# Dividing the softmax's exponentials by their sum on GpSimd instead of VectorE, in a cross-attention block of float32 products

## The chip, the core and the metric

The kernel is one program on one core of one Trainium2 chip. The metric is the device time of one execution in microseconds (us); before the change its median over 3 runs is 2565.36 us (2563.90 to 2565.37).

## The reference: what is computed

The input is x of 8 x 256 x 512 and a context of the same size, both float32. A first block (phi, theta, g and w are 1x1 convolutions, then a fixed batch normalisation) gives a new x without a softmax. Then come two cross-attention layers with 16 heads of size 128 and an MLP of width 2048, each behind a layer norm and each added to x. The part that the change touches is the softmax of the attention:

```
qh = (q_in @ wq + bq).reshape(b, q_len, H, K)
kh = concatenate([(kv_in @ wk + bk)..., bias_k]);  vh = concatenate([(kv_in @ wv + bv)..., bias_v])
logits  = einsum('bqhk,bthk->bhqt', qh, kh) / sqrt(K)
weights = softmax(logits, axis=-1)
ctx     = einsum('bhqt,bthk->bqhk', weights, vh)
return ctx.reshape(b, q_len, H * K) @ wo + bo
```

There are 256 queries and 256 keys (and one bias key) for each pair of a batch element and a head.

## The kernel before

**Products in two parts.** Each float32 operand is held as two tensors, `_hi` (rounded to the fast matmul's format) and `_lo` (what is left), and each product is three matmuls: hi*hi, lo*hi, hi*lo (`product`, L488 to L492). So whoever makes an operand makes it twice: ScalarE writes the `_hi` part out of PSUM, and VectorE then writes the `_lo` part as a difference.

**Loops.** The batch is worked on in 2 halves of 4 elements (8 tiles of 128 tokens). A half runs the first block, then 2 layers of 8 bodies, then 8 MLP bodies. An attention body handles two heads; it is one of FIRST, MIDDLE (6 of the 8), LAST and FINAL, so that the kernel has 24 MIDDLE bodies and 8 others. FIRST and LAST or FINAL also hold half of a layer norm each.

**Items.** A body has 8 items, one for each head and batch element, numbered j = 0 to 7. An item goes through these steps:

- L_j on TensorE: the logits into `S` (L639)
- the row maximum `mx` (L1015) and its negative multiple `nm` (L1017) on VectorE
- two exponentials on ScalarE into `probs`, with the row sums (L805)
- `divide` on VectorE: one reciprocal of the sums into `rs` (L1023), then for each of two tiles of 128 queries a multiplication of `probs` by `rs` (L1026), 128x256 each
- T_j on TensorE: four transposes of `probs` into `T` (L647), which wait for the semaphore a_prob
- `PT_hi` on ScalarE (L813) and `PT_lo` on VectorE (L1031)
- P_j on TensorE: the product with the values into `O`, which waits for `PT_lo` (L655)
- `oT_hi` on ScalarE (L818) and `oT_lo` on VectorE (L1037)

**Filler.** Between these steps TensorE computes units, the projections of the next operands: q, k, v for this body, K and V for the next, and w, the output product that is added to x (L1004). For a v unit VectorE adds a bias into `tmp` (L948), ScalarE makes `v_hi` and VectorE `v_lo` (L952). The order is written out by hand in a string for each kind of body, and every engine follows it in its own queue, without exceptions. A piece of it for MIDDLE, where each u is half a unit:

```
MIDDLE: "uuuu L0 uuu L1 T0 uu P0 u L2 T1 uu P1 u L3 T2 uu P2 u L4 T3 uu P3 u L5 T4 ..."
```

VectorE takes an item's steps so: at T_j it makes PT_lo of item j and then divides item j+1, and at L_j it takes the maximum of item j.

**GpSimd** (POOL) splits the weights: for each of wos, wks, wvs and wqs a cast of 128x1024 (L399) and a subtraction of 128x1024 (L401), when the last unit that reads the old weights is done and the load has landed. For wvs a third operation makes the value bias `vb` (L406). SyncE loads the next weights into `raw_ok` and `raw_vq` when a split is done. In the bodies with a layer norm GpSimd also computes the reciprocal standard deviation (`rsqrt`, L417) and adds the output bias to four tiles of x (`add_bias`, L424); VectorE makes the normalised `z` (L908) and `hT_lo` (L969) there.

Of the kernel before, what the change touches and what calls it, by code (L numbers as in the profile page):

```python
# [30 lines left out]
ALU = mybir.AluOpType  # L31
# [21 lines left out]
ITEMS = 8  # L53
# [4 lines left out]
FIRST, MIDDLE, LAST, FINAL = range(4)  # L58
# [9 lines left out]
def units_of(kind):  # L68

    return [u for u in UNITS_A if kind != FINAL or u[0] not in "KV"]  # L70


def per_body(what, kind=MIDDLE):

    return sum(u[0] in what for u in units_of(kind))


def before(half, e, what):

    return half * ((HBODIES - 1) * per_body(what) + per_body(what, FINAL)) + e * per_body(what)  # L80
# [97 lines left out]
def bass_xattn(nc, x_in, ctx_in, thw, thb, pgw, pgb, www, bncol, wa, wk, wv, wb, hcol, vrow,  # L178
               lncol, f1col, orow, out):
    ctx = ExitStack()  # L180
    with ctx:
        def sb(name, shape, dt=F32):
            return ctx.enter_context(nc.sbuf_tensor(name, [P, *shape], dt))
# [5 lines left out]
        def sem(name):  # L189
            return ctx.enter_context(nc.semaphore(name))  # L190

        def f(ap):

            return ap.bitcast(F32)
# [28 lines left out]
        probs = sb("probs", [2, 2, 258])  # L223
# [19 lines left out]
        rs = sb("rs", [2, 2])  # L243
# [41 lines left out]
        a_rawmax, a_max, a_exp, a_rcp, a_prob = (sem("a_" + s) for s in ("rawmax", "max", "exp", "rcp", "prob"))  # L285
# [25 lines left out]
        def wait_apart(eng, sem, value):  # L311


            eng.wait_ge(sem, value)
            eng.sem_inc(apart, 1)
# [65 lines left out]
        def _(pool):  # L381
# [11 lines left out]
            def as_out(raw):  # L393
                return raw[:].rearrange("p (c a) n -> p c (a n)", c=2)

            def halve(hi_lo, raw, m, count, hi_count):

                wait_apart(pool, raw_in[m], count)
                pool.tensor_copy(hi_lo[0][:], raw).then_inc(hi_part, 1)  # L399
                pool.wait_ge(hi_part, hi_count)  # L400
                return pool.tensor_tensor(hi_lo[1][:], raw, f(hi_lo[0][:]), ALU.subtract)  # L401

            def halve_v(done, hi_count):

                halve(wvs, raw_vq[:], "v", done * 32, hi_count)
                return pool.tensor_tensor(vb[:], raw_vb[:, 0, :], raw_vb[:, 1, :], ALU.subtract)  # L406
# [7 lines left out]
            def rsqrt(l, p):  # L414

                pool.wait_ge(ln_eps, l * 2 + p + 1)
                pool.tensor_tensor(rstd[:], vpe[:], minus_half[:], ALU.pow).then_inc(ln_rstd, 1)  # L417

            def add_bias(l, p):

                pool.wait_ge(brow_in, l * 16 + 16)
                for t in range(4 * p, 4 * p + 4):
                    pool.wait_ge(ln_z, l * TILES + t + 1)
                    pool.tensor_tensor(x[:, t, :], x[:, t, :], brow[:], ALU.add).then_inc(ln_bias, 1)  # L424

            def attention(half, layer, g, kind):
                e = layer * BODIES + g
                n = pool.snap(half * HBODIES + e)
                E = pool.snap(half * STREAM + e)
                hi0 = pool.snap(half * HI_HALF + e * 4 + HI0)  # L430
                l = half * NORMS + layer
                units = units_of(kind)
                ub = pool.snap(before(half, e, ALL))
                if kind == FIRST:
                    rsqrt(l, 1)

                pool.wait_ge(a_unit, ub + CR1)
                pool.wait_ge(m_unit, half * (MUNITS * MBODIES) + CR1)
                halve(wos, as_out(raw_ok), "o", E * 16 + 16, hi0 + 1).then_inc(split["o"], 1)
                if kind == FIRST:  # L440
                    add_bias(l, 1)

                pool.wait_ge(a_unit, ub + units.index(("k", 1, 1)) + 1 + CR1)
                halve(wks, raw_ok[:], "k", n * 16 + 32, hi0 + 2).then_inc(split["k"], 1)
                pool.wait_ge(a_free, ub + units.index(("v", 1, 1)) + 1 + CR4)
                halve_v(n + 2, hi0 + 3).then_inc(split["v"], 1)
                pool.wait_ge(a_unit, ub + units.index(("q", 1, 1)) + 1 + CR1)
                halve(wqs, raw_vq[:], "q", E * 16 + 32, hi0 + 4).then_inc(split["q"], 1)
                if kind >= LAST:
                    rsqrt(l + 1, 0)  # L450
                    add_bias(l + 1, 0)

            def mlp(half, g, first):
# [421 lines left out]
        def _(dve):  # L875
# [95 lines left out]
            def attention(half, layer, g, kind):  # L971
                e = layer * BODIES + g
                n = half * HBODIES + e
                units = units_of(kind)
                ub = dve.snap(before(half, e, ALL))
                jb = dve.snap(n * ITEMS)
# [42 lines left out]
                def divide(j):  # L1019

                    r = j % 2
                    dve.wait_ge(a_exp, jb + j + 1 + CR1)
                    dve.reciprocal(rs[:, r, :], sums[:, r, :]).then_inc(a_rcp, 1)  # L1023
                    dve.wait_ge(a_rcp, jb + j + 1)
                    for qt in range(2):
                        ins = dve.tensor_scalar(probs[:, r, qt, 0:256], probs[:, r, qt, 0:256], rs[:, r, qt:qt + 1], None, ALU.mult)  # L1026
                    ins.then_inc(a_prob, 1)

                def turned_lo(j):
                    dve.wait_ge(a_pthi, jb + j + 1)  # L1030
# [143 lines left out]
```

## Time and profile before

| What | us |
|---|---|
| Median of 3 runs | 2565.36 |
| Span of the profiled execution | 2566.3 |
| TensorE busy | 2423.5 (94%) |
| VectorE busy | 1779.8 (69%) |
| ScalarE busy | 914.0 (36%) |
| GpSimd busy | 668.0 (26%) |
| The two multiplications, 512 of them, on VectorE | 356.1 busy, 737 ns each on average |

The span runs from the first to the last instruction of one profiled execution, and it is 0.9 us above the median of the timed runs. The mean clock granted to TensorE over it is 0.983 of full speed. A matmul's recorded duration is longer than the distance to the next one, because matmuls are pipelined; where TensorE waits, the row says for how long and for whom, in brackets. The letter j of an item is not in the rows: it is read from the order of the rows in a body.

### The profile page before, as it was taken

The page shows a single profiled execution, that of the slowest core. Times are in us where ns is not written, and L with a number is a line of the kernel's source. Part 1 is how long each engine was busy: PE and PEld are TensorE (multiplying, and loading weights), DVE is VectorE, ACT ScalarE, POOL GpSimd, SP SyncE. Part 2 cuts the span into 40 slices and gives each one's busy share as a digit, 9 for nine tenths or more (in the row PEclk, how much of TensorE's full clock was granted, in tenths as well). Part 3 has the DMA queues.
Part 4 walks back from the last instruction along what each step waited for, and adds up shares of the span by engine and source line. Part 5 has one row for each costly group of instructions (what it writes and reads, how often), then busy time and mean ns, then how long its engine had stood idle before and what let it go on. Part 6 is the DMA issues. An engine that isn't in the chain of part 4 may idle for free.

```text
span 2566.3 us, 42151 instructions
## 1 busy us (share of the span) xinstructions
PE 2423.5 (94%) x13840; PEld 2099.5 (82%) x13840; DVE 1779.8 (69%) x3330; ACT 914.0 (36%) x2142; POOL 668.0 (26%) x427
## 2 busy tenths in 40 slices
PE   7899999998999999889999999999889999997898
PEld 5788888887888888668878888888778888886787
DVE  5777777777777777765557767777877767777555
ACT  3433333344333333411144333334343333334110
POOL 3322222223222222333312222222322222223332
PEclk9999999999999999989999999999999999999999
DMA  3111111111111111101301111111011111110111
GB/s 131 38 38 37 37 37 37 41 38 38 38 37 37 37 37 41 34 33 49 133 35 38 38 37 43 39 37 41 30 38 38 37 37 43 39 41 26 41 49 57
DMA packets 37509, 110.76 MB, mean 43 GB/s; under 512 B 4272, under 2 KB 5168, under 8 KB 37424
## 3 DMA queue, kind: packets, MB, share of 16 engines
q1 hardware_dynamic: 35312, 105.49, 12.2%
q10 hardware_dynamic: 2112, 4.19, 0.4%
q8 instruction: 46, 0.75, 0.1%
q14 instruction: 39, 0.32, 0.0%
HBM read 105.48 MB, written 4.19 MB: 43 GB/s over the span
## 4 chain that ended last, share of the span: by engine, by line
PE 70%; DVE 12%; issue 11%; ACT 4%; POOL 1%; DMA 1%; DVEq 0%; ACTq 0%; SPq 0%; POOLq 0%; PEldq 0%
PE U L490 18%; PE U L491 18%; PE U L492 18%; PE T L647 3%; DVE probs L1026 3%; PE S L490 2%; PE S L492 2%; PE S L491 2%; PE O L490 2%; DVE mx L1015 2%; PE O L491 2%; PE O L492 2%; ACT probs L805 2%; DVE z L908 1%; DVE qT_lo L988 1%
## 5 line engine op out<-in xcount | busy, mean ns | idle before, releaser
L1026 DVE TENSOR_SCALAR probs<-probs,rs 128x256 f32<-128x256 f32 x512 | 356.1, 737 | 9.0
L490 PE MATMUL U<-wos_hi,oT_hi 128*128 128x512 f32 x768 | 310.2, 404 | 12.3 <-DVE oT_lo L1094 6.9
L805 ACT ACTIVATE probs<-S,nm 128x257 f32<-128x257 f32 x512 | 238.9, 472 | 192.8 <-DVE nm L1017 191.9
L491 PE MATMUL U<-wos_lo,oT_hi 128*128 128x512 f32 x768 | 305.4, 398 | 0.0
L492 PE MATMUL U<-wos_hi,oT_lo 128*128 128x512 f32 x768 | 303.8, 396 | 0.0
L490 PE MATMUL U<-hT_hi,wqs_hi 128*128 128x512 f32 x768 | 303.4, 395 | 0.0
L492 PE MATMUL U<-hT_hi,wqs_lo 128*128 128x512 f32 x768 | 300.8, 392 | 0.0
L491 PE MATMUL U<-hT_lo,wqs_hi 128*128 128x512 f32 x768 | 300.5, 391 | 0.0
L490 PE MATMUL U<-wvs_hi,cT_hi 128*128 128x256 f32 x1024 | 298.0, 291 | 0.0
L491 PE MATMUL U<-wvs_lo,cT_hi 128*128 128x256 f32 x1024 | 289.9, 283 | 0.0
L492 PE MATMUL U<-wvs_hi,cT_lo 128*128 128x256 f32 x1024 | 289.8, 283 | 0.0
L399 POOL CAST wos_hi<-raw_ok 128x1024 fp32r<-128x1024 f32 x48 | 50.0, 1041 | 831.6 <-PE U L492 831.6
L813 ACT ACTIVATE PT_hi<-T 128x512 fp32r<-128x512 f32 x256 | 152.6, 596 | 283.0 <-PE T L647 282.9
L490 PE MATMUL U<-cT_hi,wks_hi 128*128 128x512 f32 x512 | 211.0, 412 | 0.0
L492 PE MATMUL U<-cT_hi,wks_lo 128*128 128x512 f32 x512 | 203.0, 396 | 0.0
L491 PE MATMUL U<-cT_lo,wks_hi 128*128 128x512 f32 x512 | 202.1, 395 | 0.0
L1004 DVE TENSOR_TENSOR x<-x,U 128x512 f32<-128x512 f32 x256 | 169.5, 681 | 46.9 <-PE U L492 45.8
L988 DVE SCALAR_TENSOR_TENSOR qT_lo<-U,hc,qT_hi 128x512 fp32r<-128x512 f32 x128 | 95.6, 747 | 150.7 <-ACT qT_hi L790 150.7
L1031 DVE TENSOR_TENSOR PT_lo<-T,PT_hi 128x512 fp32r<-128x512 f32 x256 | 175.7, 686 | 33.8 <-ACT PT_hi L813 32.8
L491 PEld LDWEIGHTS U<-wvs_lo,cT_hi 128*128 128x128 f32 x1024 | 196.2, 192 | 1.3
L490 PEld LDWEIGHTS U<-wvs_hi,cT_hi 128*128 128x128 f32 x1024 | 195.9, 191 | 1.1
L490 PE MATMUL O<-PT_hi,v_hi 128*128 128x256 f32 x512 | 150.3, 293 | 48.5 <-DVE PT_lo L1031 48.5
(100 smaller groups left out, 5498.6 us busy)
## 6 DMA issues: line engine op xcount, KB each, us to landing
raw_vq<-wa SPq DMA_DIRECT2D x49, 512.0 KB, 3.3
raw_ok<-wb SPq DMA_DIRECT2D x48, 512.0 KB, 4.5
raw_ok<-wk SPq DMA_DIRECT2D x33, 512.0 KB, 3.2
raw_vq<-wv SPq DMA_DIRECT2D x33, 512.0 KB, 3.3
raw_vb<-vrow SPq DMA_DIRECT2D x33, 256.0 KB, 3.5
c<-ctx_in SPq DMA_DIRECT2D x8, 512.0 KB, 7.6
x<-x_in SPq DMA_DIRECT2D x8, 512.0 KB, 8.4
out<-x ACTq DMA_DIRECT2D x4, 1024.0 KB, 5.4
```

What stands on the lines that cost most here:

```text
L399: pool.tensor_copy(hi_lo[0][:], raw).then_inc(hi_part, 1)
L490: pe.matmul(o, lhs[0], rhs[0], start=start, stop=False)
L491: pe.matmul(o, lhs[0], rhs[1], start=False, stop=False)
L492: return pe.matmul(o, lhs[1], rhs[0], start=False, stop=stop)
L647: mm = pe.transpose(T[:, tt, qt * P:qt * P + P], probs[:, j % 2, qt, tt * P:tt * P + P], ident[:])
L805: ins = act.activation(probs[:, j % 2, qt, 0:257], S[:, qt, 0:257], ACT.Exp, bias=nm[:, j % 2, qt:qt + 1], scale=SCALE, accum_out=sums[:, ...
L813: act.activation(PT[0][:], T[:], ACT.Copy).then_inc(a_pthi, 1)
L988: ins = dve.scalar_tensor_tensor(out=qslot(1, i), in0=bank(c), scalar=hc[:, 0, bass.ds(head + i, 1)], in1=f(qslot(0, i)), op0=ALU.add, op1 ...
L1004: ins = dve.tensor_tensor(x[:, t, :], x[:, t, :], bank(c), ALU.add)
L1015: dve.tensor_reduce(mx[:, j % 2, :], S[:, :, 0:257], AX.X, ALU.max).then_inc(a_rawmax, 1)
L1026: ins = dve.tensor_scalar(probs[:, r, qt, 0:256], probs[:, r, qt, 0:256], rs[:, r, qt:qt + 1], None, ALU.mult)
L1031: dve.tensor_tensor(PT[1][:], T[:], f(PT[0][:]), ALU.subtract).then_inc(a_pt, 1)
```

## The change

The two multiplications of `divide` leave VectorE. Its queue keeps the reciprocal. GpSimd gets a function `scale_probs(j)`, which waits for the reciprocal (semaphore a_rcp), multiplies both tiles of `probs` and raises a_prob for TensorE. It is called eight times in a body: for items 0 and 1 behind the split of wos, for 2 behind that of wks, for 3 behind that of wvs, and for 4 to 7 behind that of wqs. In the bodies with a layer norm `add_bias` now comes behind items 0 and 1 (FIRST), or behind item 7 (LAST, FINAL), and `rsqrt` of LAST and FINAL stands between items 6 and 7.

```diff
+                def scale_probs(j):
+
+                    r = j % 2
+                    wait_apart(pool, a_rcp, jb + j + 1)
+                    for qt in range(2):
+                        ins = pool.tensor_scalar(probs[:, r, qt, 0:256], probs[:, r, qt, 0:256], rs[:, r, qt:qt + 1], None, ALU.mult)
+                    ins.then_inc(a_prob, 1)
+
                 halve(wos, as_out(raw_ok), "o", E * 16 + 16, hi0 + 1).then_inc(split["o"], 1)
+                scale_probs(0)
+                scale_probs(1)
                 if kind == FIRST:
                     add_bias(l, 1)
 
                 pool.wait_ge(a_unit, ub + units.index(("k", 1, 1)) + 1 + CR1)
                 halve(wks, raw_ok[:], "k", n * 16 + 32, hi0 + 2).then_inc(split["k"], 1)
+                scale_probs(2)
                 pool.wait_ge(a_free, ub + units.index(("v", 1, 1)) + 1 + CR4)
                 halve_v(n + 2, hi0 + 3).then_inc(split["v"], 1)
+                scale_probs(3)
                 pool.wait_ge(a_unit, ub + units.index(("q", 1, 1)) + 1 + CR1)
                 halve(wqs, raw_vq[:], "q", E * 16 + 32, hi0 + 4).then_inc(split["q"], 1)
+                for j in range(4, ITEMS - 1):
+                    scale_probs(j)
                 if kind >= LAST:
                     rsqrt(l + 1, 0)
+                scale_probs(ITEMS - 1)
+                if kind >= LAST:
                     add_bias(l + 1, 0)
...
                     dve.reciprocal(rs[:, r, :], sums[:, r, :]).then_inc(a_rcp, 1)
-                    dve.wait_ge(a_rcp, jb + j + 1)
-                    for qt in range(2):
-                        ins = dve.tensor_scalar(probs[:, r, qt, 0:256], probs[:, r, qt, 0:256], rs[:, r, qt:qt + 1], None, ALU.mult)
-                    ins.then_inc(a_prob, 1)
```

GpSimd's queue in a MIDDLE body, before, from the split of wks to that of wqs (each wait is a semaphore's name; a_unit counts finished units, a_free units taken out of PSUM):

```order
L314 ISA [waits a_unit]
L399 CAST wks_hi<-raw_ok 128x1024 [waits raw_in_k]
L400 REGISTER_ALU
L401 TENSOR_TENSOR wks_lo<-raw_ok,wks_hi 128x1024 [waits hi_part]
L445 REGISTER_ALU
L314 ISA [waits a_free]
L399 CAST wvs_hi<-raw_vq 128x1024 [waits raw_in_v]
L400 REGISTER_ALU
L401 TENSOR_TENSOR wvs_lo<-raw_vq,wvs_hi 128x1024 [waits hi_part]
L406 TENSOR_TENSOR vb<-raw_vb 128x256
```

The same stretch now:

```order
L401 TENSOR_TENSOR wks_lo<-raw_ok,wks_hi 128x1024 [waits hi_part]
L314 REGISTER_ALU
L441 TENSOR_SCALAR probs<-probs,rs 128x256 [waits a_rcp]
L441 TENSOR_SCALAR probs<-probs,rs 128x256
L458 REGISTER_ALU
L314 ISA [waits a_free]
L399 CAST wvs_hi<-raw_vq 128x1024 [waits raw_in_v]
L400 REGISTER_ALU
L401 TENSOR_TENSOR wvs_lo<-raw_vq,wvs_hi 128x1024 [waits hi_part]
L406 TENSOR_TENSOR vb<-raw_vb 128x256
L314 REGISTER_ALU
L441 TENSOR_SCALAR probs<-probs,rs 128x256 [waits a_rcp]
```

Item 2 stands between the splits of wks and wvs, and item 3 behind the split of wvs and `vb`; each waits there for VectorE's reciprocal.

VectorE's queue in a MIDDLE body, before, from the division of item 2 to that of item 3 and the q unit behind it:

```order
L1023 RECIPROCAL rs<-sums 128x2
L1026 TENSOR_SCALAR probs<-probs,rs 128x256 x2
L997 REGISTER_ALU
L948 TENSOR_TENSOR tmp<-U,vb 128x512
...
L952 TENSOR_TENSOR v_lo<-tmp,v_hi 128x512
L1037 SCALAR_TENSOR_TENSOR oT_lo<-O,hc,oT_hi 128x256
L1015 TENSOR_REDUCE mx<-S 128x2
L1017 TENSOR_SCALAR nm<-mx 128x2
L1031 TENSOR_TENSOR PT_lo<-T,PT_hi 128x512
```

The same stretch now:

```order
L1041 RECIPROCAL rs<-sums 128x2
L1015 REGISTER_ALU
L966 TENSOR_TENSOR tmp<-U,vb 128x512
...
L970 TENSOR_TENSOR v_lo<-tmp,v_hi 128x512
L1051 SCALAR_TENSOR_TENSOR oT_lo<-O,hc,oT_hi 128x256
L1033 TENSOR_REDUCE mx<-S 128x2
L1035 TENSOR_SCALAR nm<-mx 128x2
L1045 TENSOR_TENSOR PT_lo<-T,PT_hi 128x512
```

Only the pair of multiplications is gone; the maximum, `nm` and `PT_lo` keep their order. The queues of TensorE, ScalarE and SyncE hold the same instructions in the same order as before.

## Rows read from the trace of the kernel before

**Rows 1.** One MIDDLE body: length, busy of PE, PEld, DVE, ACT, POOL, clock, DMA.
```profile
264.34:326.06 61.72, 60.40 (x369) 53.44 (x368) 44.33 (x89) 24.02 (x60) 14.52 (x10) 1.00 0.11 38
```

**Rows 2.** Waits of TensorE in that body: total us, times, longest.
```profile
PE O L490 <- DVE PT_lo L1031: 1.0, 1, 1.0
PE S L490 <- DVE qT_lo L988: 0.4, 1, 0.4
```

**Rows 3.** Timeline of TensorE in that body: T0, P1, T2, P2, T3, T4.
```profile
274.97 0.60 PE L647 MATMUL T<-ident,probs 128*128 128x128 f32 x4
...
285.53 0.39 PE L490 MATMUL O<-PT_hi,v_hi 128*128 128x256 f32 x1 [0.95 <-DVE PT_lo L1031]
...
288.44 0.60 PE L647 MATMUL T<-ident,probs 128*128 128x128 f32 x4
...
291.62 0.28 PE L490 MATMUL O<-PT_hi,v_hi 128*128 128x256 f32 x1
...
295.08 0.60 PE L647 MATMUL T<-ident,probs 128*128 128x128 f32 x4
...
301.16 0.60 PE L647 MATMUL T<-ident,probs 128*128 128x128 f32 x4
```

**Rows 4.** Timeline of GpSimd in that body: the splits of wks, wvs and wqs.
```profile
277.22 1.04 POOL L399 CAST wks_hi<-raw_ok 128x1024 fp32r<-128x1024 f32 x1 [9.36 <-PE U L492]
...
289.04 1.04 POOL L399 CAST wvs_hi<-raw_vq 128x1024 fp32r<-128x1024 f32 x1 [8.29 <-DVE v_lo L952]
290.16 2.41 POOL L401 TENSOR_TENSOR wvs_lo<-raw_vq,wvs_hi 128x1024 fp32r<-128x1024 f32 x1
292.52 0.79 POOL L406 TENSOR_TENSOR vb<-raw_vb 128x256 f32<-128x256 f32 x1
296.72 1.04 POOL L399 CAST wqs_hi<-raw_vq 128x1024 fp32r<-128x1024 f32 x1 [3.41 <-DMA raw_vq<-wa]
```

**Rows 5.** Timeline of VectorE in that body, items 0 to 3.
```profile
273.25 0.17 DVE L1023 RECIPROCAL rs<-sums 128x2 f32<-128x2 f32 x1 [1.09 <-ACT probs L805]
...
275.16 0.69 DVE L1015 TENSOR_REDUCE mx<-S 128x2 f32<-128x514 f32 x1 [0.29 <-PE S L492]
...
277.15 0.17 DVE L1023 RECIPROCAL rs<-sums 128x2 f32<-128x2 f32 x1 [0.23 <-ACT probs L805]
277.35 3.54 DVE L1026 TENSOR_SCALAR probs<-probs,rs 128x256 f32<-128x256 f32 x2
...
286.70 0.69 DVE L948 TENSOR_TENSOR tmp<-U,vb 128x512 f32<-128x512 f32 x1
288.09 0.69 DVE L952 TENSOR_TENSOR v_lo<-tmp,v_hi 128x512 fp32r<-128x512 f32 x1 [0.70 <-ACT v_hi L798]
...
289.81 0.29 DVE L1017 TENSOR_SCALAR nm<-mx 128x2 f32<-128x2 f32 x1
```

**Rows 6.** Timelines of VectorE and TensorE in one FIRST body, items 3 and 4.
```profile
1890.48 2.05 DVE L1017 TENSOR_SCALAR nm<-mx 128x2 f32<-128x2 f32 x1
...
1898.07 2.20 DVE L1017 TENSOR_SCALAR nm<-mx 128x2 f32<-128x2 f32 x1
...
1900.91 0.39 PE L490 MATMUL O<-PT_hi,v_hi 128*128 128x256 f32 x1 [1.38 <-DVE PT_lo L1031]
```

**Rows 7.** Two source lines over the span: durations in ns, min/median/max.
```profile
L1026 DVE TENSOR_SCALAR probs<-probs,rs x512: 342/354/2599, 81.9 to 2355.6; 128x256 f32<-128x256 f32 x171
L406 POOL TENSOR_TENSOR vb<-raw_vb x33: 738/788/820, 28.6 to 2326.9; 128x256 f32<-128x256 f32 x33
```

**Rows 8.** Largest sum of waits of TensorE over the whole span.
```profile
PE O L490 <- DVE PT_lo L1031: 48.5, 41, 3.8
```

**Rows 9.** Timelines of VectorE (FIRST, LAST) and GpSimd (LAST) in layer norms.
```profile
587.48 6.62 DVE L908 TENSOR_SCALAR z<-x,mv,rstd 128x512 f32<-128x512 f32 x4 [0.43 <-POOL rstd L417]
...
561.09 3.83 DVE L908 TENSOR_SCALAR z<-x,mv,rstd 128x512 f32<-128x512 f32 x4
...
561.71 5.55 POOL L424 TENSOR_TENSOR x<-x,brow 128x512 f32<-128x512 f32 x4 [0.66 <-DVE z L908]
```

More of the change, by code:

```diff
@@ L433, in attention @@
                 ub = pool.snap(before(half, e, ALL))
+                jb = pool.snap(n * ITEMS)
+                def scale_probs(j):
[4 more added lines that the diff above has]
+                    ins.then_inc(a_prob, 1)
                 if kind == FIRST:
```

## The prediction, on record before the changed kernel ran

> **What bounds the kernel now.** I read the totals first, then one MIDDLE body, because 24 of the 32 attention bodies are alike. In such a body TensorE is busy 60.40 of 61.72 us and VectorE 44.33 [rows 1], so TensorE sets the pace and VectorE matters only where TensorE waits for it. The waits by engine give two such places, 1.0 us for `PT_lo` and 0.4 us for `qT_lo` [rows 2]. The timeline puts the first at P1, 0.95 us at 285.53 [rows 3]. Its cause is visible on VectorE: the pair of multiplications of item 1 starts at 277.35 and takes 3.54 us [rows 5], while GpSimd casts from 277.22 and then subtracts for the split of wks [rows 4]. Undisturbed, one multiplication takes 0.35 us; the longest took 2.6 [rows 7]. So VectorE stands still while GpSimd works, and what is queued behind (the v unit, the maximum of item 2, `PT_lo` of item 1) comes late. Over the span the waits for `PT_lo` are 48.5 us in 41 places [rows 8], and a MIDDLE body holds one of them.
>
> **What is removed.** 512 multiplications with a mean of 737 ns, a median of 354: some 356 us of VectorE's time go, of which (737 - 354) ns x 512 = 196 us were blocking. Almost none of that is on TensorE's path, which can win only its own waits. In a MIDDLE body these are 0.95 + 0.4 = 1.3 us (the second, at L4, has the same cause, the blocked pair of item 3), and 24 x 1.3 = 31 us is the most that these bodies can give.
>
> **What is added.** GpSimd gets 256 pairs. No row shows this operation there. The nearest with one input, a cast of 128x1024, takes 1.04 us [rows 4], a quarter of which is 0.26; the nearest in shape, a subtraction of 128x256 with two inputs, takes 0.79 [rows 7]. A multiplication lies between 0.26 and 0.79 us; I take 0.40, nearer the cast since it has one large input. A pair is then 0.8 us, and it begins about 0.2 us behind the reciprocal (the cast of wvs begins 0.26 us behind the end of `v_lo` at 288.78). I now walk through the queue of a MIDDLE body, by the clock of the old trace.
>
> - Item 0: the reciprocal ends at 273.42 [rows 5], the pair at 274.4 (at 275.2 with 0.79 us). T0 starts at 274.97 [rows 3]: nothing lost (0.3 us at the far end).
> - Item 1: pair from 277.5 to 278.3. The split of wks, queued behind it, moves from 277.2 to 278.4 and ends at 282.0. Its readers, the K units, come behind item 3. VectorE is now free at once instead of at 277.35 + 3.54 = 280.9. It takes `tmp` of the first v unit as TensorE finishes it (about 280.6), reaches `v_lo` 1.4 us later as between 286.70 and 288.09 [rows 5], just when the split ends, then needs 0.6 for it, 0.7 each for the maximum and `PT_lo` and 0.1 for `nm`: `PT_lo` of item 1 is ready near 284.1, before the 285.53 - 0.95 = 284.6 at which TensorE wants it. The 0.95 us at P1 go.
> - `v_lo` of the second v unit, at 288.09 before, comes 2.0 us earlier, near 286.1: 0.95 because TensorE is earlier and the rest because nothing delays `tmp` (286.70 before). The split of wvs depends on it, so its subtraction moves from 290.16 to about 288.2, and `vb` ends near 291.3.
> - Item 3: T2 moves to 288.44 - 1.1 = 287.3. The maximum follows 0.19 us behind a T, `nm` 0.72 behind that (275.16 against 274.97), so `nm` of item 3 comes at 288.2. This is the doubtful place: `nm` is a small multiplication, and it too stands still beside GpSimd. At 289.81 it took 0.29 us instead of 0.17, until the cast ended, and slipped in before the subtraction [rows 5]. In one FIRST body it came 0.36 us behind the start of the subtraction and took 2.05 [rows 6]. Here cast end and `nm` fall within 0.1 us. If GpSimd's pair of item 1 takes longer than 0.8 us, `v_lo` and with it this split come later, and `nm` slips in more safely. I take it that it does.
> - Item 3's pair follows `vb`, 291.4 to 292.2; T3 is due at 295.08 - 1.3 = 293.8. Nothing lost.
> - Item 4: the load of wqs takes 3.4 us from the split of wvs, so the cast moves from 296.72 to 294.8 and the subtraction ends at 298.4. The pair behind it ends at 299.3 (300.1 at the far end), T4 is due at 301.16 - 1.3 = 299.9. Nothing lost, up to 0.2.
> - Items 5 to 7 find GpSimd idle.
>
> A MIDDLE body so gains 1.3 less about 0.1 for small waits: 1.2 us, 29 us over 24.
>
> **The layer norms.** In LAST and FINAL `z` takes 3.83 us because `add_bias` runs beside it (561.71, four tiles, 5.55 us) [rows 9]. That now comes behind item 7. Four operations at the 0.69 us of an undisturbed 128x512 [rows 5] would be 2.8 at most, so 1 to 1.7 us go; but `add_bias` then falls upon `hT_lo`, which can give most of it back. I take 1 us for each of 4 bodies (0 to 1.7). In FIRST, `z` takes 6.62 us beside the split of wos and `add_bias` [rows 9]; it should end some 1.5 us earlier, but `add_bias` then stands beside `hT_lo` and pushes the split of wks back by 5.5 us in front of item 2. I take 0 for each of 4 (gain or loss of 2).
>
> **Sum**, against the profiled execution: 2566.3 - 29 - 4 = 2533.3. Its span is 0.9 us above the median of the runs, so the time is 2532.4; I say 2533.
>
> **A rule against it.** The row shows VectorE's 0.35 us multiplication lasting as long as GpSimd's subtraction [rows 5, 7]. The Trainium skill, "SBUF — State Buffer", section Who interferes with whom, says the same: VectorE in a two-port mode, or with two SBUF inputs, and GpSimd lock each other out of one shared port pair, and PSUM inputs don't count. Its "Perfetto Trace Analysis", section Optimizing Scalar/DVE Operations, concludes that moving work between these two might not help. By that, time would merely move from the pair to `nm` and `v_lo`, which is the first rival below. The skill's "GPSIMD Engine Reference", section 3.1, gives 1.03 cycles an element for a simple one-input loop, at 1.2 GHz 0.22 us for 256: an estimate that no run here shows and that would leave the sum as it is.
>
> **Rivals.**
> 1. The block moves to `nm`. If `nm` of item 3 comes just behind the start of the subtraction, it is held until 290.6, `PT_lo` of item 2 ends at 291.2, and P2, due at 291.62 - 1.1 = 290.5, waits 0.7. P2 is then tied to the end of that subtraction, and `nm` of item 4 to P2; the FIRST body of rows 6 runs so, and there `nm` of item 4 is caught too (2.20 us) and P3 waits 1.38. The 1.3 us gained become 2.1 us of new waits: 24 x 0.8 = 19 us slower, less 4: 2580. For it: the rows just named, and a distance under 0.1 us. Against it: before, `nm` slips in, and a longer pair on GpSimd helps it. It decides from the point where `nm` of item 3 starts behind the subtraction.
> 2. Only item 3 is caught and item 4 slips in before its subtraction: 1.3 - 0.7 = 0.6 us a body, 14 in all, with the norms 18: 2547.
> 3. GpSimd's multiplication is slow, 0.8 to 1.2 us. Then T0 is 0.3 to 1 us late, P1 again waits for VectorE behind a later split, and T4 is 0.2 to 1 us late: the gain is eaten up, 2560 to 2580. For it: the two-input row of 0.79. Against it: the cast.
> 4. The change does not do what it says: not so, the order shows the pair in the other queue. That it is hidden anyway can't be, since TensorE's two waits end with VectorE.
>
> **Numbers.** Forecast 0.52; rival 2 0.13; rival 1 0.22; rival 3 0.13, of which 0.08 within 0.2% and 0.05 slower. That makes faster by over 0.2% (5 us, about what a measurement of this kernel can tell from none) 0.65, the same 0.08, slower 0.27. The range runs from 2517 (all that MIDDLE bodies can give, 34 with the slower first matmul behind a wait, 8 in FIRST, 7 in LAST and FINAL) to 2584 (rival 1 with nothing won in the norms). The forecast's own range is 2517 to 2545.
>
> **What the new profile would show.** Right: in a MIDDLE body of about 60.5 us no wait at P1 and L4; a multiplication of about 0.4 us on GpSimd; `nm` of item 3 at most 0.4 us long; the cast of wvs 2 us earlier against its body. Wrong: `nm` with 2 us in many bodies and TensorE waiting at P2 and P3 for `PT_lo` (rival 1); T waiting for `probs` of GpSimd (rival 3); a split late enough that a unit waits for its weights, which I hold excluded; more than 2 us lost in a FIRST body.

## The result, and the profile after

The changed kernel takes 2572.8 us (median of 6 runs, 2564.59 to 2577.86), the kernel before 2565.16 (6 runs, 2563.9 to 2566.04). The ratio is 1.0028, with a 95% interval of 1.0018 to 1.0038: slower by 0.3%, where 2533 was forecast. The first profile is of the execution that took 2564.59, the fastest of the six; a second profile, of a run near the median (2574.33), is used beside it. Of the kernel before, one execution in the last group of experiments took 13462 us, for a reason that no profile shows; it is in no ratio and no range here.

The page of the first profile. VectorE is busy 273 us less than before, GpSimd 473 us more:

```profile
span 2562.8 us, 42663 instructions
## 1 busy us (share of the span) xinstructions
PE 2423.7 (95%) x13840; PEld 2092.1 (82%) x13840; DVE 1506.4 (59%) x2818; ACT 912.6 (36%) x2142; POOL 1140.9 (45%) x939
```

The source line of the multiplication on GpSimd, with its durations in ns (min/median/max), and who waited for it:

```profile
L441 POOL TENSOR_SCALAR probs<-probs,rs x512: 915/927/1451, 76.6 to 2352.1; 128x256 f32<-128x256 f32 x171
...
  PEld T L665: 72.0, 96
  PE T L665: 52.0, 71
```

It takes 927 ns at the median, where VectorE takes 354 undisturbed [rows 7]. TensorE, which before hardly ever waited for `probs`, now does so 71 times. One MIDDLE body, the one that answers to [rows 1], first as a row of busy times, then its waits of TensorE:

```profile
261.58:323.56 61.98, 60.76 (x369) 53.50 (x368) 36.11 (x73) 23.96 (x60) 29.05 (x25) 1.00 0.11 38
```

```profile
PE T L665 <- POOL probs L441: 1.0, 2, 0.5
PE O L508 <- DVE PT_lo L1045: 0.3, 1, 0.3
```

Of the waits of [rows 2], the one for `qT_lo` is gone and 0.3 us of the one for `PT_lo` is left. Two new ones stand at T0 and T4. TensorE's timeline shows them; the rows are T0, T2, T3 and T4:

```profile
272.78 0.66 PE L665 MATMUL T<-ident,probs 128*128 128x128 f32 x4 [0.42 <-POOL probs L441]
...
285.61 0.60 PE L665 MATMUL T<-ident,probs 128*128 128x128 f32 x4
...
291.77 0.66 PE L665 MATMUL T<-ident,probs 128*128 128x128 f32 x4
...
298.62 0.66 PE L665 MATMUL T<-ident,probs 128*128 128x128 f32 x4 [0.54 <-POOL probs L441]
```

Against the start of its own body (264.34 before, 261.58 now), T0 comes at 11.20 us (10.63 before), T2 at 24.03 (24.10), T3 at 30.19 (30.74), T4 at 37.04 (36.82). So the body loses 0.57 up to T0, gains 0.64 from there to T2 and 0.48 to T3, and loses 0.77 between T3 and T4. GpSimd's timeline shows why: the pair of item 0, the pair of item 3 and the split of wqs with the pair of item 4 behind it:

```profile
270.86 1.86 POOL L441 TENSOR_SCALAR probs<-probs,rs 128x256 f32<-128x256 f32 x2 [5.76 <-DVE rs L1041]
...
289.89 1.82 POOL L441 TENSOR_SCALAR probs<-probs,rs 128x256 f32<-128x256 f32 x2
293.21 1.04 POOL L399 CAST wqs_hi<-raw_vq 128x1024 fp32r<-128x1024 f32 x1 [1.49 <-DMA raw_vq<-wa]
294.34 2.41 POOL L401 TENSOR_TENSOR wqs_lo<-raw_vq,wqs_hi 128x1024 fp32r<-128x1024 f32 x1
296.72 1.84 POOL L441 TENSOR_SCALAR probs<-probs,rs 128x256 f32<-128x256 f32 x2
```

The pair of item 0 ends at 272.72 and T0 starts at 272.78. The pair of item 4 ends at 298.56 and T4 starts at 298.62. On average over the 24 MIDDLE bodies (from one cast of wos to the next) a body takes 62.18 us, against 61.69 before, and 62.20 in the second profile. The others, two halves each, in us:

| Bodies | before | after, run of 2564.59 | after, run of 2574.33 |
|---|---|---|---|
| MIDDLE, mean of 24 | 61.69 | 62.18 | 62.20 |
| FIRST, mean of 4 | 68.65 | 68.41 | 68.72 |
| LAST, mean of 2 | 75.81 | 73.07 | 74.35 |
| FINAL, mean of 2 | 73.21 | 69.23 | 71.49 |

The MIDDLE bodies cost 24 x 0.5 = 12 us in both; LAST and FINAL give back 13 us in the run of 2564.59 and 6 in the other. In the run near the median that leaves 6 us, which is the difference of the two spans (2572.5 and 2566.3). How much of what LAST and FINAL give back is the granted clock is worked out under "The changed kernel once more".

### The profile page after: what moved, and what is told of

Same layout as the page of the kernel before. It is cut to its first block, busy times and chain, and to the rows that moved or that the text cites. A ratio compares the mean times of both kernels' runs of the same rounds, so it can differ in the third digit from the quotient of the medians.

```text
span 2562.8 us, 42663 instructions
## 1 busy us (share of the span) xinstructions
PE 2423.7 (95%) x13840; PEld 2092.1 (82%) x13840; DVE 1506.4 (59%) x2818; ACT 912.6 (36%) x2142; POOL 1140.9 (45%) x939
## 4 chain that ended last, share of the span: by engine, by line
PE 60%; POOL 11%; DVE 10%; issue 10%; ACT 5%; DMA 4%; POOLq 0%; ACTq 0%; DVEq 0%; SPq 0%; PEldq 0%
PE U L508 16%; PE U L509 16%; PE U L510 16%; POOL probs L441 5%; DMA raw_vq<-wa 3%; PE T L665 3%; DVE v_lo L970 3%; ACT probs L823 2%; DVE mx L1033 2%; DVE tmp L966 2%; PE O L508 2%; ACT v_hi L816 2%; PE O L509 1%; PE O L510 1%; POOL wvs_lo L401 1%
## 5 line engine op out<-in xcount | busy, mean ns | idle before, releaser
L441 POOL TENSOR_SCALAR probs<-probs,rs 128x256 f32<-128x256 f32 x512 | 470.9, 930 | 692.5 <-DVE rs L1041 692.5
L665 PE MATMUL T<-ident,probs 128*128 128x128 f32 x1024 | 159.5, 278 | 52.2 <-POOL probs L441 52.0
L1033 DVE TENSOR_REDUCE mx<-S 128x2 f32<-128x514 f32 x256 | 176.0, 688 | 48.2 <-PE S L510 47.0
```

What stands on the lines that cost most here:

```text
L441: ins = pool.tensor_scalar(probs[:, r, qt, 0:256], probs[:, r, qt, 0:256], rs[:, r, qt:qt + 1], None, ALU.mult)
L665: mm = pe.transpose(T[:, tt, qt * P:qt * P + P], probs[:, j % 2, qt, tt * P:tt * P + P], ident[:])
L1033: dve.tensor_reduce(mx[:, j % 2, :], S[:, :, 0:257], AX.X, ALU.max).then_inc(a_rawmax, 1)
```

## The experiments

Each was run beside the kernel before on the same chip, and each ratio is to that. Differences in us to the changed kernel go by its 2572.8 of another group of runs; the median of the kernel before was between 2563 and 2565.2 us in all groups.

**Item 0 back on VectorE.**

```diff
+                    if j == 0:
+                        dve.wait_ge(a_rcp, jb + j + 1)
+                        for qt in range(2):
+                            ins = dve.tensor_scalar(probs[:, r, qt, 0:256], ...)
+                        ins.then_inc(a_prob, 1)
...
-                scale_probs(0)
```

> The changed kernel, with the pair of multiplications of item 0 back on VectorE; items 1 to 7 stay on GpSimd. Theory: a multiplication takes GpSimd 0.93 us, not 0.40, so a pair takes 1.83 where VectorE took 0.62, and two places of a MIDDLE body can't hide the difference: T0, which starts 0.57 us later against its body than before (11.20 against 10.63 us behind the cast of wos), and T4. If so, T0 comes back to 10.6, a MIDDLE body loses 0.3 to 0.57 us, and the time falls from 2572.8 by 8 to 18 us. Rival: T0 is late for another reason (VectorE's small casts beside GpSimd), then T0 stays at 11.1 or later and the time falls by under 3 us.

It took 2545.65 us, ratio 0.9935 (0.9923 to 0.9948). T0 and T4 in one body that starts at 260.88, from TensorE's timeline:

```profile
271.50 0.60 PE L664 MATMUL T<-ident,probs 128*128 128x128 f32 x4
...
297.40 0.66 PE L664 MATMUL T<-ident,probs 128*128 128x128 f32 x4 [0.66 <-POOL probs L441]
```

T0 is at 10.62 again, and T4 still waits. The theory holds; the gain of 27 us is larger than the 8 to 18 expected. A MIDDLE body has 61.49 us, 0.7 less than in the changed kernel (17 us over 24), and the bodies with a layer norm give the rest: they are 11 us shorter than in the changed kernel's second profile.

**The pair of item 4 ahead of the split of wqs.**

```diff
                 scale_probs(3)
+                scale_probs(4)
                 pool.wait_ge(a_unit, ub + units.index(("q", 1, 1)) + 1 + CR1)
                 halve(wqs, raw_vq[:], "q", E * 16 + 32, hi0 + 4).then_inc(split["q"], 1)
-                for j in range(4, ITEMS - 1):
+                for j in range(5, ITEMS - 1):
```

> The changed kernel, with the pair of item 4 ahead of the split of wqs in GpSimd's queue instead of behind it. Theory: the split waits for its load (3.3 to 3.7 us from issue to landing), and the pair of item 4 and so T4 wait behind both; between T3 and T4 a MIDDLE body loses 0.77 us or more against before, and since the load's duration differs from execution to execution, so does the kernel's time (2564.6 to 2577.9). If so, the time falls by 15 to 30 us to about 2550, and its runs spread over 3 us or less. Rival: the spread and the loss come from something else (the clock in the FIRST bodies, the block of nm), then the time changes by under 5 us and the spread stays at 10 us.

It took 2539.97 us, ratio 0.9908 (0.9894 to 0.9922). T0 and T4 in a body that starts at 259.20:

```profile
270.38 0.66 PE L666 MATMUL T<-ident,probs 128*128 128x128 f32 x4 [0.41 <-POOL probs L441]
...
295.50 0.60 PE L666 MATMUL T<-ident,probs 128*128 128x128 f32 x4
```

Here T0 waits as in the changed kernel and T4 comes at 36.30 without a wait. The place of the loss is confirmed, 1.0 us a MIDDLE body (61.20); the gain of 33 us is a little over the 15 to 30 expected. The half of the theory on the spread is not confirmed: these four runs still lie between 2531.8 and 2541.2.

**Both at once.** The edit is the sum of the two.

> Item 0 on VectorE and the pair of item 4 ahead of the split of wqs, both at once. Theory: the two losses are at different places and add up; a MIDDLE body comes to 60.6 to 61.0 us, and the time to 2535 to 2545, below the kernel before. Rival: VectorE's or GpSimd's other blocks (nm beside a subtraction, v_lo beside the split of wks, 1.41 us) take up what is won; then the time is no better than that of the better of the two edits alone.

It took 2518.88 us, ratio 0.9824 (0.9811 to 0.9836), and its five runs are within 1 us. T0 and T4 in a body that starts at 259.38:

```profile
270.00 0.60 PE L665 MATMUL T<-ident,probs 128*128 128x128 f32 x4
...
295.09 0.60 PE L665 MATMUL T<-ident,probs 128*128 128x128 f32 x4
```

T0 at 10.62 and T4 at 35.71. Alone the two edits gain 27 and 33 us, together 54, and a MIDDLE body takes 60.63. The time lies below the 2535 to 2545 expected. So the same change, with two pairs placed otherwise, is 45 us faster than the kernel before (2563.98 in this group).

**Half the columns.** GpSimd multiplies 128 of 256 columns; the other half stays undivided.

```diff
-    ins = pool.tensor_scalar(probs[:, r, qt, 0:256], probs[:, r, qt, 0:256], rs[:, r, qt:qt + 1], None, ALU.mult)
+    ins = pool.tensor_scalar(probs[:, r, qt, 0:128], probs[:, r, qt, 0:128], rs[:, r, qt:qt + 1], None, ALU.mult)
```

> The changed kernel, with GpSimd multiplying only 128 of the 256 columns of each tile, the other half of the probabilities left undivided. It measures the operation's fixed part and how its duration matters. If its time goes with the elements, 128x128 takes 0.5 us; if most of it is fixed, 0.8. Theory: with 0.5 us both T0 and T4 lose their waits for probs (T4 only partly, since the split of wqs still stands ahead of it) and the time falls by 15 to 32 us to about 2550. Rival: the pair's duration is not what costs, then under 5 us.

It took 2504.44 us, ratio 0.9769 (0.9756 to 0.9782).

```profile
L441 POOL TENSOR_SCALAR probs<-probs,rs x512: 595/607/639, 76.5 to 2289.5; 128x128 f32<-128x128 f32 x171
```

From 607 to 927 ns for 128 more elements a partition is 2.5 ns an element, and a line through the two points leaves 0.29 us fixed. The pair's duration is what costs: 1.2 instead of 1.83 us gives 68 us, far above the 15 to 32 expected, and more than the places T0 and T4 gave together (54). A MIDDLE body has 60.07 us. The third place is P1: in the version with both edits TensorE still waits 0.26 us there for `PT_lo`, here not at all, and T2 comes at 22.88 us of its body against 23.42. That is 0.54 us, 13 over 24 bodies, and 54 + 13 = 67.

In one body `nm` of item 3, from VectorE's timeline, starts only just ahead of GpSimd's subtraction for wvs:

```profile
280.26 0.17 DVE L1035 TENSOR_SCALAR nm<-mx 128x2 f32<-128x2 f32 x1
```

```profile
280.30 2.40 POOL L401 TENSOR_TENSOR wvs_lo<-raw_vq,wvs_hi 128x1024 fp32r<-128x1024 f32 x1
```

In the 24 MIDDLE bodies this distance is 0.02 to 0.08 us, and `nm` takes 0.17 each time. So this time rests on a few hundredths of a microsecond, as the next versions show.

**The changed kernel once more.**

> The changed kernel once more, for its spread and a second profile. Its six runs lay between 2564.6 and 2577.9, with the profile in the fastest of them, while the version with item 4 ahead of the split of wqs ran within 2531.8 to 2541.2 and the one with both edits within 1 us. Theory: the load of wqs is on the path of T4, so that a slower execution has MIDDLE bodies that differ among each other by the landing of that load, and a mean body above 62.2 us. Rival: the MIDDLE bodies are the same 62.2 and the time differs in the FIRST, LAST and FINAL bodies or the first block.

It took 2572.7 us (9 runs, 2566.87 to 2575.11), ratio 1.0031 (1.0020 to 1.0041). The theory falls and the rival holds: the MIDDLE bodies are the same in both profiles (62.18 and 62.20), and the difference is in the layer norm bodies of the table above, which are 8.3 us longer together in the second. One LAST and one FINAL body, as length, busy times and, third from the end, the granted clock; first the kernel before, then the run of 2564.59, then that of 2574.33:

```profile
511.18:587.40 76.22, 70.13 (x405) 61.75 (x404) 57.70 (x116) 29.91 (x69) 22.05 (x16) 0.96 0.09 32
1024.99:1098.18 73.19, 61.08 (x333) 52.20 (x332) 53.49 (x105) 28.08 (x66) 22.00 (x15) 0.93 0.09 30
```

```profile
509.93:583.01 73.08, 67.58 (x405) 58.99 (x404) 48.62 (x100) 29.98 (x69) 36.48 (x32) 1.00 0.10 33
1024.98:1094.20 69.22, 58.44 (x333) 50.01 (x332) 42.58 (x89) 28.24 (x66) 37.88 (x32) 0.98 0.10 31
```

```profile
514.06:588.40 74.34, 69.11 (x405) 60.52 (x404) 47.93 (x100) 29.95 (x69) 35.97 (x31) 0.98 0.10 33
1029.42:1101.63 72.21, 61.38 (x333) 52.45 (x332) 42.56 (x89) 28.07 (x66) 37.01 (x31) 0.93 0.10 30
```

Time at 1.2 instead of 2.4 GHz counts half in the granted clock. So 0.93 over 73.19 us means 2 x 0.07 x 73.19 = 10 us at the lower level. Added up over the eight bodies with a layer norm, it is 57 us before, 30 in the run of 2564.59 and 48 in that of 2574.33. The 18 us between the last two cost half of that, 9 us, where TensorE works throughout, and 8.3 were measured. The spread follows the clock, too: the two fastest of the 15 executions of the changed kernel (2564.59 and 2566.87) were granted 0.989, all others 0.985 to 0.987, and of the version with item 4 ahead of the split of wqs the execution of 2531.81 had 0.989, the three around 2540 had 0.985 or 0.986. What makes the clock fall in one execution and not in another stays open: over the span, TensorE's largest waits are nearly the same in both profiles (52.0 and 51.5 us for `probs`, 29.0 and 29.7 for `PT_lo`, 20.6 and 20.6 for `z`).

The same holds for the comparison with before. The 14 us by which the eight bodies are shorter in the run of 2564.59 come with 27 us less at 1.2 GHz, worth up to 13; the 6 us in the run of 2574.33 come with 9 us less, worth up to 4.5. Whether the change itself keeps the clock up is not shown.

**No multiplication at all.** The two multiplications are left out and the probabilities stay undivided; everything else is as before.

```diff
-                    dve.reciprocal(rs[:, r, :], sums[:, r, :]).then_inc(a_rcp, 1)
-                    dve.wait_ge(a_rcp, jb + j + 1)
-                    for qt in range(2):
-                        ins = dve.tensor_scalar(probs[:, r, qt, 0:256], ...)
-                    ins.then_inc(a_prob, 1)
+                    dve.reciprocal(rs[:, r, :], sums[:, r, :]).then_inc(a_prob, 1)
```

> The kernel before, with the two multiplications left out altogether (the probabilities stay undivided), and add_bias where it was. It shows how much the multiplications cost as they stood, wherever they are put. Theory: VectorE's pair, blocked by GpSimd's splits, was what TensorE waited for in MIDDLE bodies, so these come to 60.1 us, as with GpSimd's half-width pairs, 1.6 x 24 = 38 us in all, and the LAST and FINAL bodies gain less than they did in the changed kernel (76 to 73 and 73 to 69 us), because add_bias has not moved: about 2522. Rival: without the pair the stand-still moves to nm (2 us in the FIRST body of the trace before), and a MIDDLE body stays above 61 us: about 2550.

It took 2529.08 us, ratio 0.9860 (0.9842 to 0.9877), between theory and rival, and slower than half of the multiplications on GpSimd. VectorE's timeline and TensorE's in one body, with `nm` of items 3 and 4 and the products P2 and P3:

```profile
282.32 2.38 DVE L1017 TENSOR_SCALAR nm<-mx 128x2 f32<-128x2 f32 x1
...
289.94 2.29 DVE L1017 TENSOR_SCALAR nm<-mx 128x2 f32<-128x2 f32 x1
```

```profile
285.34 0.39 PE L490 MATMUL O<-PT_hi,v_hi 128*128 128x256 f32 x1 [0.61 <-DVE PT_lo L1027]
...
292.88 0.39 PE L490 MATMUL O<-PT_hi,v_hi 128*128 128x256 f32 x1 [1.21 <-DVE PT_lo L1027]
```

GpSimd's subtractions start at 282.28 and 289.82 there, 0.04 and 0.12 us ahead of `nm`:

```profile
282.28 2.39 POOL L401 TENSOR_TENSOR wvs_lo<-raw_vq,wvs_hi 128x1024 fp32r<-128x1024 f32 x1
...
289.82 2.39 POOL L401 TENSOR_TENSOR wqs_lo<-raw_vq,wqs_hi 128x1024 fp32r<-128x1024 f32 x1
```

This body takes 62.20 us, and the mean of the MIDDLE ones is 61.04 (60.70 to 62.29). It is the mechanism of the prediction's rival 1. `nm` of item 3 starts 0.03 to 0.05 us behind the subtraction in all 24 MIDDLE bodies and is held in each; that of item 4 is held in 5 of them. In the changed kernel `nm` of item 3 starts 0.26 to 0.29 us ahead of the subtraction, in both profiles, and is never held; with half of the columns it is 0.02 to 0.08. The 1.0 us by which a MIDDLE body is longer here than with half of the columns lies behind T2 (22.88 in both bodies), at P2 and P3. No run moves `nm` alone.

**Only `add_bias` moved.** The multiplications are on VectorE.

```diff
                 if kind == FIRST:
+                    pool.wait_ge(a_rcp, jb + 2)
                     add_bias(l, 1)
...
                     rsqrt(l + 1, 0)
+                    pool.wait_ge(a_rcp, jb + ITEMS)
                     add_bias(l + 1, 0)
```

> The kernel before with its multiplications on VectorE, and only add_bias moved to where the change puts it: behind the reciprocal of item 1 in FIRST, behind that of item 7 in LAST and FINAL. In the changed kernel a LAST body fell from 76 to 73 and a FINAL body from 73.2 to 69.2 us. Theory: that is the move of add_bias, which no longer blocks z; then this kernel gains 3 to 4 us in each of these 4 bodies, 12 to 15 in all, with MIDDLE bodies at 61.7: about 2551. Rival: it is the freed VectorE, then LAST and FINAL stay within 1 us of before.

It took 2552.03 us, ratio 0.9954 (0.9934 to 0.9975), as expected; but where the gain lies was not. `z` in LAST, from VectorE's timeline:

```profile
555.81 1.92 DVE L911 TENSOR_SCALAR z<-x,mv,rstd 128x512 f32<-128x512 f32 x4
```

It takes 1.92 us instead of 3.83 [rows 9]. Yet LAST falls only from 75.81 to 74.73 and FINAL from 73.21 to 70.92; FIRST falls from 68.65 to 65.73, which neither theory named. MIDDLE bodies stay at 61.70. The clock has a part in this as well: the eight bodies are 18 us shorter than before, with 25 us less at 1.2 GHz, worth up to 12. Among executions with the same granted clock of 0.986 the gain is 8 to 10 us (2556.07 here, 2563.99 to 2565.86 before), so the move is worth something by itself. The changed kernel has this move inside. Its FIRST bodies lose by the rest of the change: with a clock of 0.97 in both, they take 65.4 to 66.5 us here and 68.0 in the changed kernel.

**The multiplications on ScalarE.**

```diff
                     ins.then_inc(a_exp, 1)
+                    act.wait_ge(a_rcp, jb + j + 1)
+                    for qt in range(2):
+                        ins = act.activation(probs[:, j % 2, qt, 0:256], probs[:, j % 2, qt, 0:256], ACT.Copy,
+                                             scale=rs[:, j % 2, qt:qt + 1])
+                    ins.then_inc(a_prob, 1)
```

> The kernel before, with the two multiplications on ScalarE (a scaled copy by the reciprocal, behind the exponentials of the same item), add_bias unmoved. ScalarE is busy 24 of 62 us in a MIDDLE body and is never held up beside GpSimd in any trace here. Theory: two copies of 128x256 at about 0.47 us hide, VectorE is as free as without the multiplications, and the time is that of the version without them plus at most 10 us: 2522 to 2535. Rival: ScalarE then makes the hi parts of k, v and q units about 1.2 us later, each time in front of VectorE's lo part, and a MIDDLE body stays at 61 to 62 us: about 2560.

It took 2503.36 us, ratio 0.9761 (0.9743 to 0.9779), better than expected and than the version without multiplications. The multiplication's group in the trace (busy us, mean ns), and one MIDDLE body:

```profile
L811 ACT ACTIVATE probs<-probs,rs 128x256 f32<-128x256 f32 x512 | 233.2, 503 | 59.6 <-DVE rs L1028 59.6
```

```profile
258.15:318.22 60.07, 60.07 (x369) 53.38 (x369) 34.76 (x73) 30.61 (x76) 14.44 (x9) 1.00 0.12 39
```

TensorE is busy all of the 60.07 us and waits for nothing. The mean of the MIDDLE bodies is 59.91. No `nm` takes over 1.1 us in the whole span: in MIDDLE bodies that of item 3 starts 0.14 to 0.34 us ahead of the subtraction. The subtraction holds `nm` in every MIDDLE body of the version without multiplications and in none here; as far as the rows show, that is why the version with less work is the slower one.

**One operation for both tiles on GpSimd.**

```diff
-                    for qt in range(2):
-                        ins = pool.tensor_scalar(probs[:, r, qt, 0:256], probs[:, r, qt, 0:256], rs[:, r, qt:qt + 1], None, ALU.mult)
+                    ins = pool.tensor_tensor(probs[:, r, :, 0:256], probs[:, r, :, 0:256],
+                                             rs[:, r, :].unsqueeze(2).to_broadcast([P, 2, 256]), ALU.mult)
```

> The changed kernel, with GpSimd's two multiplications by a column (927 ns each, 128x256, 1.83 us a pair) replaced by one tensor by tensor multiplication of 128x512 against the column spread out. The kernel before shows GpSimd's two-input subtraction of 128x256 at 0.79 us and its addition of 128x512 at 1.25 to 1.44. Theory: the duration of the pair is what costs, and one operation of about 1.3 us takes half a us off T0 and T4: a MIDDLE body falls from 62.2 to about 61.3, and the time from 2572.8 to 2545 to 2555. Rival: a spread column is read as slowly as it is with the multiplication by a column, so that 128x512 takes 1.6 us or more and the time stays above 2560.

```profile
L440 POOL TENSOR_TENSOR probs<-probs,rs x256: 1031/1042/1052, 78.9 to 2328.4; 128x512 f32<-128x512 f32 x128
```

It took 2543.59 us (2535.77 to 2550.73), ratio 0.9921 (0.9904 to 0.9938), just below the range expected. One operation of 1.04 us does what took 1.83. With this edit alone the changed kernel is faster than before, and T waits 7.7 us for `probs` over the span instead of 52.0. But a MIDDLE body still takes 61.36 us on average, and up to 62.30, because now rival 1 of the prediction is there. VectorE's `nm` of items 3 and 4 in one body of 62.24 us, the two subtractions of GpSimd, and P2 and P3 of TensorE:

```profile
285.63 2.37 DVE L1035 TENSOR_SCALAR nm<-mx 128x2 f32<-128x2 f32 x1
...
293.26 2.33 DVE L1035 TENSOR_SCALAR nm<-mx 128x2 f32<-128x2 f32 x1
```

```profile
285.59 2.39 POOL L401 TENSOR_TENSOR wvs_lo<-raw_vq,wvs_hi 128x1024 fp32r<-128x1024 f32 x1
...
293.19 2.38 POOL L401 TENSOR_TENSOR wqs_lo<-raw_vq,wqs_hi 128x1024 fp32r<-128x1024 f32 x1
```

```profile
288.65 0.38 PE L508 MATMUL O<-PT_hi,v_hi 128*128 128x256 f32 x1 [0.61 <-DVE PT_lo L1045]
...
296.24 0.39 PE L508 MATMUL O<-PT_hi,v_hi 128*128 128x256 f32 x1 [1.25 <-DVE PT_lo L1045]
```

`nm` of item 3 is held so in all 24 MIDDLE bodies, that of item 4 in 10.

**The same in the version with both edits.**

> The same one operation of 128x512, in the version with item 0 on VectorE and item 4 ahead of the split of wqs (2518.9). Theory: there T hardly waits for probs any more (7.4 us in 10 places), but a shorter pair lets the split of wks end earlier, which holds v_lo (1.41 us in a MIDDLE body of the changed kernel) and so PT_lo of item 1: a MIDDLE body falls from 60.63 to about 60.3, the time to 2508 to 2515. Rival: an earlier split meets nm as in the version without multiplications (2.38 us in most MIDDLE bodies), and the time rises to 2520 to 2530.

It took 2511.49 us, ratio 0.9796 (0.9783 to 0.9809), inside the expected range, but not for the reason given: its MIDDLE bodies are not shorter (60.73 against 60.63). What the rival named did happen: `nm` of item 3 takes 2.38 us in all 24 of them and P2 waits 0.62, which takes back what is won at P1. LAST and FINAL are shorter, by 2.7 and 3.2 us, in part by the clock; among executions at 0.987 the gain is 5 to 7 us (2511.44 and 2513.17 against 2518.34).

**ScalarE, and `add_bias` moved.** The two edits at once.

> Multiplications on ScalarE (2503.4) and add_bias moved (alone 12 us better). Theory: the two are at different places, MIDDLE bodies stay at 59.9, and the FIRST, LAST and FINAL bodies lose some 10 us together: 2490 to 2496. Rival: with ScalarE busier, the layer norm's chain over ScalarE (aff, hT_hi) is what ends last in those bodies, and the two add up to less than 5 us: 2498 or more.

It took 2499.29 us, ratio 0.9745 (0.9732 to 0.9758), the best of all and 2.6% under the kernel before, but only 4 us under ScalarE alone: the rival's price. MIDDLE bodies are at 59.95. LAST and FINAL fall from 73.1 to 70.3 and from 67.9 to 65.6, while FIRST rises from 66.7 to 67.8. At a granted clock of 0.986 the two versions take 2500.55 and 2501.06, so that even the 4 us may be the clock. That the chain over ScalarE is the cause there was not shown.

## Why the prediction was wrong

**The step that failed** is the price of the multiplication on GpSimd: "between 0.26 and 0.79 us; I take 0.40". It is 0.93, outside even the bounds. What the prediction called "nothing lost" at T0 and T4 thereby became 0.57 and 0.77 us a MIDDLE body, and a gain of 29 us over these bodies became a loss of 12. The range was bounded by a row with one input and four times the elements, and by one with two inputs of the same shape, as if an operation with fewer large inputs had to be quicker. The multiplication by a column does not follow that: it goes at 2.5 ns an element, where the cast takes 1.04 us for 1024 elements (1.0 ns each), and the same product as tensor by tensor over 512 columns takes 1.04. The sentence on 1.03 cycles an element for a simple one-input loop in the Trainium skill, "GPSIMD Engine Reference", section 3.1, does not fit this operation: it makes 0.22 us of 256 elements, as the prediction worked out, where 0.93 was measured. The measurement decides.

**What hung on it.** At 0.79 the prediction made T0 0.3 us late and T4 up to 0.2. At 0.93, T0 is 0.57 later and T4 0.77 later than the step before it, which is more than the waits printed (0.42 and 0.54), so a printed wait doesn't hold the whole delay. Both places were named, and two experiments with one edit each and one with both show them to be the ones: 27, 33 and 54 us. The outcome is rival 3, given a chance of 0.13 and 2560 to 2580 us. That the time lies inside the stated range of 2517 to 2584 is by this rival, not by the forecast's mechanism.

**The most that MIDDLE bodies can give** was put at 1.3 us each, from the waits of [rows 2]. With ScalarE it is 61.69 - 59.91 = 1.8. So printed waits were a lower bound. The rows of T show where the rest is. T2, T3 and T4 in the body with ScalarE, which starts at 258.15:

```profile
281.01 0.60 PE L647 MATMUL T<-ident,probs 128*128 128x128 f32 x4
...
287.03 0.60 PE L647 MATMUL T<-ident,probs 128*128 128x128 f32 x4
...
293.33 0.60 PE L647 MATMUL T<-ident,probs 128*128 128x128 f32 x4
```

Against the start of the body T2 comes at 22.86 (24.10 before), T3 at 28.88 (30.74) and T4 at 35.18 (36.82). So 1.24 us are won up to T2, where the wait at P1 was printed as 0.95, and 0.62 from T2 to T3, where 0.4 was printed; 0.22 are lost again up to T4.

**`nm` of item 3** was rightly the doubtful place. It slipped in, but for a reason that the forecast did not have. VectorE's timeline in the changed kernel, items 3 and 4:

```profile
286.54 0.22 DVE L1035 TENSOR_SCALAR nm<-mx 128x2 f32<-128x2 f32 x1
...
293.30 0.98 DVE L1035 TENSOR_SCALAR nm<-mx 128x2 f32<-128x2 f32 x1
```

The longer pair of item 1 had moved the splits back, the way the prediction said it would. With shorter pairs the margin goes: `nm` starts 0.26 to 0.29 us ahead of the subtraction with a pair of 1.83 us, 0.02 to 0.08 ahead with one of 1.2, and 0.03 to 0.05 behind it, held for 2.4 us in all 24 MIDDLE bodies, with one of 1.04 and with no multiplication at all. The forecast's own pair of 0.8 us lies between the last two and was not run; by these neighbours `nm` would have been caught. So had the price of 0.40 been right, rival 1 or 2 would have been likelier than the forecast, and the assumption that `nm` slips in held by luck. The price of rival 1 was well sized, 0.7 and 1.38 us at P2 and P3, where the version with one operation shows 0.61 and 1.25; but not its time of 2580: `nm` of item 4 is caught in only 10 of the 24 bodies, and that version took 2543.59.

**The waits at P1 and L4** went nearly as said, from 0.95 to 0.3 and from 0.4 to nothing. The 0.3 that stay come from `v_lo`, which was expected to be just in time for the end of the split of wks and stood still beside it for 0.7 us, since at 0.93 the pair of item 1 lasts 1.83 us and ends only at 277.21:

```profile
275.38 1.83 POOL L441 TENSOR_SCALAR probs<-probs,rs 128x256 f32<-128x256 f32 x2 [2.66 <-DVE rs L1041]
277.16 1.04 POOL L399 CAST wks_hi<-raw_ok 128x1024 fp32r<-128x1024 f32 x1
278.29 2.40 POOL L401 TENSOR_TENSOR wks_lo<-raw_ok,wks_hi 128x1024 fp32r<-128x1024 f32 x1
```

```profile
279.83 1.41 DVE L970 TENSOR_TENSOR v_lo<-tmp,v_hi 128x512 fp32r<-128x512 f32 x1 [0.70 <-ACT v_hi L816]
```

So a part of VectorE's standing still came back in another operation: `v_lo` takes 116.8 us over the span, 88.7 before.

**The layer norms** were sized better than the table suggests. The forecast was 1 us for each LAST and FINAL and 0 for FIRST. The table shows 2.7 and 4.0 in the run of 2564.59, but there a LAST and a FINAL body together spent 10 us less at 1.2 GHz than before. Bodies with the same granted clock, before and in the run of 2574.33, give 75.39 and 74.35 for LAST (0.98), 73.19 and 72.21 (0.93) and 73.22 and 70.77 (0.95) for FINAL: 1.0, 1.0 and 2.5 us. FIRST is near 0, as said, made of a gain with `add_bias` moved and a loss by the rest. That `z` could go down to 2.8 us "at most" was from a row of another operation; it goes to 1.92. `hT_lo` was hit by `add_bias` as forecast: its mean over the span rises from 768 to 1078 ns.

**The spread** was not foreseen. Over all groups of runs the kernel before lies within 7 us (2560.80 to 2568.02), the changed kernel within 13 (2564.59 to 2577.86).

## What to carry to other kernels

Work that is moved to an engine with time to spare is paid for in latency, at each place where someone waits, not in busy time: here GpSimd had 74% of its time free, and 1.2 us more a pair cost more than 273 us of relief brought. Put the moved step in the new queue ahead of every long operation that nobody waits for, and keep the steps without slack where they were; that turned 0.3% slower into 1.8% faster. And when two engines hold each other up, look for a third: ScalarE, slower at the multiplication than VectorE undisturbed, made the kernel 2.4% faster. But look in each version at the small operation that may start just before or just behind a long one of the other engine: here less than 0.1 us decided over 2.2 us of standing still in every MIDDLE body, and with it, as far as the rows show, over some 25 us of the whole.

## What the runs showed of the hardware

- GpSimd multiplies 128x256 float32 by a column in 0.93 us and 128x128 in 0.61; 128x512 tensor by tensor against a spread-out column takes 1.04 us, 0.8 us less than the two of 128x256 together.
- A VectorE multiplication of 128x2, 0.17 us alone, takes 2.3 to 2.4 us when it starts 0.03 to 0.12 us behind the start of a GpSimd subtraction of 128x1024, and 1.4 when it starts 1.0 us behind: it stands until the subtraction ends. When it starts during the cast ahead, it takes up to 1.05 us, until the cast ends, and slips in before the subtraction.
- `v_lo`, a subtraction with two inputs in SBUF, took 1.41 us instead of 0.69 beside GpSimd's subtraction; `nm`, `z`, `v_lo` and `hT_lo` were held up so in these traces; `PT_lo`, with one input in PSUM, never took over 0.69 us in any of them, and ScalarE's multiplication took 0.49 to 0.52 us in all 512 cases.
- Two executions of one program with the same MIDDLE bodies differed by 9.7 us in their spans, with a mean granted clock of 0.989 and 0.986; in the bodies with a layer norm, where 8.3 us of it lie, 30 and 48 us were spent at 1.2 GHz.
